# An attention and feed-forward block on one core: iterations written out, weight splits spread over iterations, rotation tables made in later groups, preparation reordered

## The chip, the cores and the metric

One NeuronCore of a Trainium2 chip. The time is device microseconds (us) of one execution. Engines by the profile's names: PE is the matrix engine (PEld its weight loads), ACT the scalar engine, DVE the vector engine, POOL GpSimd, SP the engine that issues most DMAs.

## The reference, cut to what matters

```python
x = x + layernorm(attn(layernorm(x)))     # x: 8 images of 512 tokens x 256
x = x + layernorm(ffn(layernorm(x)))
# attn, 16 heads of 64 complex numbers; t is the token
q, k, v = complex projections of x;  qr, kr = q * phase, k * phase   # phase = exp(i * t * omega)
E = exp(clip(-mu * |t_i - t_j|, -30, 0))
s = real(qr @ conj(kr));  qn, kn = |q|^2, |k|^2
V = sigma2 / (2 mu) * (1 - E * E) + eta2 + gamma2
maha = max(qn + E*E*kn - 2*E*s, 0) / V
logits = -0.5*tau*(nu+64) * log1p(maha / nu) - 32 * log(V), causal
out = softmax(logits) @ v;  y = out @ Wo
# ffn: silu(x @ Wg) * (x @ Wu) @ Wd, 256 -> 768 -> 256, integer weights
```

Everything is in float32. A projection is made from three products of high and low parts, so weights and inputs are split into `hi` (rounded to the matrix engine's format) and `lo = x - hi`.

## The kernel before, in words

The 16 heads are taken in 8 groups of 2 heads; a group goes over the 8 images. One *iteration* is one image in one group, 64 in all, numbered t. An iteration's program is software-pipelined: each engine, in a fixed order written by hand in its `body`, works on the present image (`c`), finishes the one before (`cp`) and begins the next (`cn`). In PE's order, an iteration has `project` (L786), `scores` (L826), `turn` (L838, transposes of the probabilities), `attend` (L850), `values` (L816) and `out_project` (L861). ACT squares projections (L1169), takes `log` (L1186) and `exp` (L1194), and copies PSUM results (`keep_turned` L1201, `keep_values` L1180, `keep_norm_k` L1175). DVE has `rotate` (L1488), `decay` (L1596), `distance` (L1607), `logits` (L1615), `add_output` (L1639). POOL has `sum_squares` (L600), `rotated` (L608) and `decay_norm` (L618). Engines meet only by semaphores; the order on each is the program's.

How the iterations are issued: `run_iterations` writes out t = 0 to 8. Groups 1 to 6 stand in an outer hardware loop of three rounds with two groups each; inside a group, iterations 1 to 4 are an inner loop of two rounds with two iterations each. Group 7 comes after the outer loop. In looped code the counts that semaphores are compared with are registers, and `settle` adds a semaphore increment on DVE ahead of each `distance` and `logits`.

A group needs its own weights and tables. SP loads the raw weights of the next group into the `lo` half of `wt` and the tables into `tabs` of the other parity. In each of the iterations j = 5 and 6 of a group, ACT turns three 256-column slots into `hi` with one instruction (`high_weights`, L374) at the start of its body, and POOL subtracts them one by one at three places (`low_weights`, L379).

The rotation tables (cos, sin, -sin of t * omega, 4 heads a set, 4 sets `ROPES`) are all made in t = 0: DVE makes the reduced angles with 5 instructions a set (L1460 to L1469), ACT the sines and cosines with 4 (L1125 to L1130), and SP stores them to DRAM, from where a group's table is loaded. Layer-norm statistics of the images (`x_stats`, L1506) are taken for images 4, 5 and 6, 7 in pairs, in t = 0 and t = 1. The feed-forward weights are cast from integers (`ffn_cast_of`, L1153, on ACT), transposed on PE (`ffn_turn`, L751) and copied out by ACT (`ffn_keep`, L1149): 9 turns, 4 of them ahead of t = 0 and 5 in it. After t = 63 the feed-forward part runs.

## Time and profile before

| | us |
|---|---|
| median of 3 runs (1907.66 to 1908.88) | 1907.91 |
| the profiled execution | 1907.7 |
| its span, first to last instruction | 1905.9 |
| PE busy | 1798.5 (94%) |
| DVE busy | 1609.2 (84%) |
| ACT busy | 1578.6 (83%) |
| POOL busy | 1453.4 (76%) |

The table is read as shares of the whole span. Stages differ: preparation up to the start of t = 0 (some 50 us), then 64 iterations, then the feed-forward part of some 190 us. The rows below cut the span into iterations, at the starts of the `values` products (L816).

### The profile page before, as it was taken

Reading aid. Unit: us, or ns where it says so; the run is one execution under the profiler, and the core shown is the slowest. Engines: PE = TensorE matmul, PEld = TensorE weight load, DVE = VectorE, ACT = ScalarE, POOL = GpSimd, SP = SyncE. Lnnn points to the kernel's source line nnn. Section 1 sums busy time; section 2 is a strip of 40 time slices with the busy share of each in tenths; the row PEclk is TensorE's granted clock in tenths of the full one; section 3 lists DMA queues with packets and bytes.
Section 4 is the critical chain, followed back from the end, with each engine's and each line's share of the span. In section 5 each row is a group of like instructions: output and inputs, shape, how many; then the busy total and the mean of one; then the engine's idle time right before and its main releaser. Section 6 shows DMA issues by size and latency. Waiting matters only on the chain.

```text
span 1905.9 us, 40909 instructions
## 1 busy us (share of the span) xinstructions
PE 1798.5 (94%) x10672; PEld 1477.9 (78%) x10672; DVE 1609.2 (84%) x3842; ACT 1578.6 (83%) x3224; POOL 1453.4 (76%) x1288
## 2 busy tenths in 40 slices
PE   4589999999999999999999999999999999998997
PEld 3377788887888887887888778887888788876876
DVE  7788898888888887888888878888888888996884
ACT  5779888898888887888888888888888888886664
POOL 5367788888888887888888877888888888872663
PEclk8799999999999999999999999999999999999998
DMA  7313101231122111311013111211131111010111
GB/s 210 119 40 111 62 24 44 78 94 45 45 78 88 33 42 47 110 62 46 33 69 94 46 47 64 89 43 46 45 111 45 46 45 42 26 54 14 45 45 45
DMA packets 61087, 117.72 MB, mean 62 GB/s; under 512 B 13488, under 2 KB 42928, under 8 KB 52704
## 3 DMA queue, kind: packets, MB, share of 16 engines
q1 hardware_dynamic: 59936, 115.51, 18.0%
q8 instruction: 78, 1.28, 0.3%
q14 instruction: 113, 0.93, 0.2%
q10 hardware_dynamic: 960, 0.00, 0.0%
HBM read 99.64 MB, written 21.36 MB: 63 GB/s over the span
## 4 chain that ended last, share of the span: by engine, by line
PE 60%; DVE 10%; POOL 8%; issue 6%; ACT 2%; DVEq 0%; POOLq 0%; ACTq 0%
PE pa L786 13%; PE ps L826 11%; PE py L850 10%; PE po L861 9%; PE pp L816 7%; PE pp L838 5%; POOL qk L608 4%; PE pa L797 3%; PE pa L805 2%; DVE lg L1607 2%; DVE stats L1645 1%; POOL ek L618 1%; DVE ps L1596 1%; DVE lg L1615 1%; DVE acc L1667 1%
## 5 line engine op out<-in xcount | busy, mean ns | idle before, releaser
L608 POOL TENSOR_TENSOR qk<-rm 64x512 f32<-64x512 f32 x504 | 684.2, 1357 | 102.7 <-PE ps L826 44.2
L618 POOL TENSOR_TENSOR ek<-tabs,kn 128x512 f32<-128x512 f32 (+3 forms) x512 | 460.7, 906 | 151.7 <-DVE lg L1607 112.1
L1615 DVE CUSTOM_DVE_ANT_0 lg<-lg,tabs,ncog 128x512 f32<-128x512 f32 (+3 forms) x512 | 442.6, 883 | 0.6 <-issue 0.6
L786 PE MATMUL pa<-xt,wt 128*128 128x512 f32 x1488 | 424.4, 421 | 12.5 <-issue 6.9
L826 PE MATMUL ps<-qk 128*128 128x512 f32 (+3 forms) x1024 | 375.0, 450 | 25.0 <-DVE lg L1607 24.9
L1488 DVE TENSOR_TENSOR rm<-pa,tabs 128x512 f32<-128x512 f32 x504 | 327.9, 678 | 70.8 <-POOL qk L608 65.7
L1607 DVE CUSTOM_DVE_ANT_0 lg<-ps,ek,qb 128x512 f32<-128x512 f32 (+3 forms) x512 | 279.5, 546 | 125.3 <-POOL ek L618 82.7
L850 PE MATMUL py<-pt,vt 128*128 128x128 f32 x2560 | 347.9, 275 | 0.1
L850 PEld LDWEIGHTS py<-pt,vt 128*128 128x128 f32 x2560 | 330.6, 191 | 16.5 <-issue 0.3
L786 PEld LDWEIGHTS pa<-xt,wt 128*128 128x128 f32 x1488 | 275.9, 193 | 66.1 <-issue 11.2
L1186 ACT ACTIVATE lg<-lg,qb 128x512 f32<-128x512 f32 (+3 forms) x512 | 278.5, 558 | 19.4 <-DVE lg L1607 15.9
L1194 ACT ACTIVATE pr<-lg,nmax 128x512 f32<-128x512 f32 (+3 forms) x512 | 283.3, 554 | 1.5
L861 PE MATMUL po<-wot,yt 128*128 128x256 f32 x1024 | 271.3, 388 | 6.1 <-DVE acc L1637 3.1
L1596 DVE TENSOR_TENSOR ps<-ps,tabs 128x512 f32<-128x512 f32 (+3 forms) x512 | 250.1, 489 | 23.8 <-PE ps L826 22.4
L1201 ACT ACTIVATE pt<-pp 128x512 f32<-128x512 f32 (+3 forms) x512 | 219.1, 430 | 59.2 <-PE pp L838 40.9
L861 PEld LDWEIGHTS po<-wot,yt 128*128 128x128 f32 x1024 | 180.3, 191 | 84.3 <-DVE acc L1639 42.2
L838 PEld LDWEIGHTS pp<-ident,pr 128*128 128x128 f32 x1280 | 164.0, 141 | 80.2 <-issue 44.0
L1639 DVE SCALAR_TENSOR_TENSOR acc<-po,rden,acc 128x256 f32<-128x256 f32 (+1 forms) x480 | 208.0, 474 | 16.4 <-PE po L861 16.4
L1169 ACT ACTIVATE sq<-pa 128x512 f32<-128x512 f32 x256 | 151.6, 593 | 82.4 <-PE pa L786 82.2
L838 PE MATMUL pp<-ident,pr 128*128 128x128 f32 x1280 | 214.2, 274 | 4.1 <-ACT pr L1194 2.3
L600 POOL TENSOR_TENSOR sq<-sq 128x512 f32<-128x512 f32 x126 | 161.9, 1285 | 54.8 <-ACT sq L1169 54.7
L826 PEld LDWEIGHTS ps<-qk 128*128 128x128 f32 x1024 | 161.0, 192 | 48.6 <-DVE lg L1607 41.1
(193 smaller groups left out, 2245.2 us busy)
## 6 DMA issues: line engine op xcount, KB each, us to landing
xt<-xs_d SPq DMA_DIRECT2D x56, 1024.0 KB, 4.8
tabs<-vec_d SPq DMA_DIRECT2D x7, 1536.0 KB, 9.6
xs_d<-xt SPq DMA_DIRECT2D x6, 1024.0 KB, 4.0
wt<-wraw_d SPq DMA_DIRECT2D x7, 768.0 KB, 5.6
acc<-in_L_attn_x SPq DMA_DIRECT2D x8, 512.0 KB, 6.0
tabs<-in_L_attn_x SPq DMA_DIRECT2D x8, 512.0 KB, 4.9
out<-tabs SPq DMA_DIRECT2D x8, 512.0 KB, 3.1
tabs<-rope_d SPq DMA_DIRECT2D x56, 64.0 KB, 4.1
```

What stands on the lines that cost most here:

```text
L608: pool.tensor_tensor(qk[part * DH:(part + 1) * DH, z * HH + hh, :], rm[row, 2 * part, :], rm[row, 2 * part + 1, :], ALU.add if part else A ...
L618: pool.tensor_tensor(ek[:, n % 2, 0:w], tab(par, hh, E2_T, w), kn[:, hh, 0:w], ALU.mult).then_inc(ek_pool, 1)
L786: last = mm(pa[r][:, :], wproj(par, z, kt, a, r * P, (r + 1) * P), xbuf[x][:, kt, b, :], start=(n == 0), stop=(n == 3 * KT - 1))
L826: mm(ps[n % 2][:, 0:w], qk[:, hh, TILES[n] * P:(TILES[n] + 1) * P], qk[:, HH + hh, 0:w], start=True, stop=True).then_inc(s_rdy, 1)
L838: last = pe.transpose(pp[i][:, j * P:(j + 1) * P], pr[:, hh, o:o + P], ident[:, :])
L850: last = mm(py[:, I * P:(I + 1) * P], vt[:, slot, j, hh * P:(hh + 1) * P], pt[:, i, j * P:(j + 1) * P], start=(j == 0), stop=(j == I))
L861: last = mm(po[:, jj * D:(jj + 1) * D], yt[:, hh, j * P:(j + 1) * P], wot[:, par, hh * D:(hh + 1) * D], start=True, stop=True)
L1186: act.activation(lg[:, hh, at(n)], lg[:, hh, at(n)], ACT.Ln, bias=qb[:, slot, 1, q:q + 1]).then_inc(ln_act, 1)
L1194: act.activation(pr[:, hh, at(n)], lg[:, hh, at(n)], ACT.Exp, bias=nmax[:, q:q + 1], scale=-1.0, accum_out=den[:, q:q + 1]).then_inc(ex_ac ...
L1488: tt(rm[:, m, :], pa[r][:, :], ropet(par, m in (IS, RS)), ALU.mult).then_inc(mul_dve, 1)
L1607: dve._custom_dve(bass.dve_ops.TENSOR_ADD_SAT, out=lg[:, hh, at(n)], in0=ps[n % 2][:, 0:w], in1=ek[:, n % 2, 0:w], s0=3e38, s1=qb[:, slot, ...
L1615: dve.tensor_tensor_reduce(lg[:, hh, at(n)], lg[:, hh, at(n)], tab(par, hh, T3_T, w), ncog[:, par, 0, hh:hh + 1], 3e38, ALU.add, ALU.min, ...
```

## The change

1. `run_iterations` writes out all 64 iterations on each engine; there are no loops, registers or `settle`. Counts are constants.
2. The weight split: one slot an iteration. ACT takes one 256-column slot after its second `log`, POOL subtracts it after `decay_norm(c, 1, 0)`. Groups 1 to 6 do this in j = 1 to 6, group 0 in j = 2 to 6 (two slots in the last). SP loads the raw weights at j = 0 (group 0: j = 1), the output weights one iteration later with a semaphore of their own.
3. Rotation tables: set 0 is made in t = 0. Sets 1, 2, 3 are made in groups 1, 3, 5, in the buffer that the next group's tables will take: DVE's five instructions in j = 1, 2, 3, ACT's sines in j = 3 and cosines in j = 4; SP stores them at j = 4, and then loads the next group's tables (before: at j = 2 and 3).
4. Preparation: `mu` is loaded and used first, the norm constants (`nco`) go out before the decay vectors, the small column arithmetic on DVE is ahead of the first rotations, `x_stats` goes by one image (images 4 to 7 in t = 0 to 3), and the feed-forward casts and turns are spread: 1 cast and 2 turns ahead of t = 0, 2 casts and 7 turns in it. The first raw weights lie in other buffers.

```diff
-        def run_iterations(eng, body):
-            for t in range(B + 1):
-                body(whole(t))
...
-            with eng.Fori(0, G // 2 - 1) as gg:
-                group(gg, 1, False)
-                group(gg, 0, False)
-            group(G // 2 - 1, 1, True)
+        def run_iterations(body):
+            for t in range(G * B):
+                g, j = divmod(t, B)
+                if g == G - 1:
+                    split = ()
+                elif g == 0:
+                    split = (j - 2,) if 2 <= j < 6 else (4, 5) if j == 6 else ()
+                else:
+                    split = (j - 1,) if 1 <= j < 7 else ()
+                if g == 0:
+                    rope = (0, 0) if j == 0 else None
+                else:
+                    rope = ((g + 1) // 2, j) if g % 2 and g < G - 1 and 1 <= j < 5 else None
...
 ACT body
-                if it.raw is not None:
-                    act.wait_ge(w_in[1 - it.par], it.raw)
-                    high_weights(act, 1 - it.par, 3 * it.part, 3 * it.part + 3).then_inc(w_hi, 1)
...
                 log(c, 0, 2, it.slot)
+                for g, q in it.split:
+                    high_weights(act, g, q)
...
                 keep_values(c, it.slot, 1)
-                if it.own == 1:
-                    for k in range(ROPES):
-                        rope_trig(k)
-                    act.wait_ge(rope_act, 4 * ROPES + 3)
+                if it.rope == (0, 0):
+                    rope_sines(0)
+                    rope_cosine(0)
+                    act.wait_ge(rope_out[0], 48)
+                elif it.rope is not None and it.rope[1] == 3:
+                    rope_sines(it.rope[0])
+                elif it.rope is not None and it.rope[1] == 4:
+                    rope_cosine(it.rope[0])
                 log(c, 1, 3, it.slot)
...
 DVE body
                 decay(c, 1, 2, it.par)
+                if it.rope is not None and it.rope[1] == 1:
+                    angle_turns(it.rope[0])
+                if it.rope is not None and it.rope[1] == 2:
+                    angle_first(it.rope[0])
+                if it.rope is not None and it.rope[1] == 3:
+                    angle_clamp(it.rope[0])
                 if nxt:
                     rotate(cn, it.behind, 1, RC)
...
-                if it.own == 1:
-                    all_angles_ready()
-                    for k in range(ROPES):
-                        rope_angle(k)
-                if it.own in (1, 2):
-                    x_stats(it.own + 2)
...
                 decay(c, 1, 3, it.par)
+                if it.own is not None and it.own < 5:
+                    x_stats(it.own + 3)
+                if it.rope is not None and it.rope[1] == 1:
+                    angle_whole(it.rope[0])
+                if it.rope is not None and it.rope[1] == 2:
+                    angle_second(it.rope[0])
                 distance(c, 1, 3, it.slot)
```

Where instructions stand. POOL, iteration j = 5 of a looped group before: the three subtractions L379 (`wt`) among `rotated` (qk), `sum_squares` (sq) and `decay_norm` (ek).

```order
L618 TENSOR_TENSOR ek<-tabs,kn 128x512 [waits x_dve]
L377 ISA
L379 TENSOR_TENSOR wt<-wt 128x256 [waits w_hi]
L599 REGISTER_ALU
L600 TENSOR_TENSOR sq<-sq 128x512 [waits sq_act]
...
L608 TENSOR_TENSOR qk<-rm 64x512 [waits s_rdy,mul_dve,rot_pool1]
L379 TENSOR_TENSOR wt<-wt 128x256 [waits w_hi,rot_pool1]
```

The same place on POOL now, in one of the iterations j = 1 to 6 of group 1: one subtraction (now L346), with no register instructions around it.

```order
L593 TENSOR_TENSOR ek<-tabs,kn 128x128 [waits x_dve,rot_pool1]
L593 TENSOR_TENSOR ek<-tabs,kn 128x512 [waits x_dve,kn_act]
L346 TENSOR_TENSOR wt<-wt 128x256 [waits w_hi]
L575 TENSOR_TENSOR sq<-sq 128x512 [waits sq_act]
L583 TENSOR_TENSOR qk<-rm 64x512 [waits s_rdy,mul_dve,sum_pool]
```

Two of the three subtractions of such an iteration have moved to other iterations; the one that stays stands ahead of `sum_squares`.

ACT at the end of an iteration in a looped group before: `exp`, `keep_values`, then `log` (1, 3) and `keep_turned` (0, 0), whose output `pt` PE's next `turn` waits for.

```order
L1194 ACTIVATE pr,den<-lg,nmax 128x512 [waits rd_dve,tr_rdy,f_dve]
L1180 ACTIVATE vt<-pp 128x512 [waits v_rdy]
L1186 ACT_TABLE_LOAD
L1186 ACTIVATE lg<-lg,qb 128x128 [waits x_dve]
L1201 ACTIVATE pt<-pp 128x512 [waits av_rdy,tr_rdy]
```

The same place now in j = 3 and then in j = 4 of group 1 (groups 3 and 5 alike): sines, and cosines by way of the absolute value, each with an activation-table load of their own.

```order
L1163 ACTIVATE vt<-pp 128x512 [waits v_rdy]
L1104 ACT_TABLE_LOAD
L1104 ACTIVATE tabs<-tabs 128x512 [waits rope_dve]
L1105 ACTIVATE tabs<-tabs 128x512
L1169 ACT_TABLE_LOAD
L1169 ACTIVATE lg<-lg,qb 128x128 [waits x_dve]
L1184 ACTIVATE pt<-pp 128x512 [waits av_rdy,tr_rdy]
...
L1163 ACTIVATE vt<-pp 128x512 [waits v_rdy]
L1111 ACTIVATE tabs<-tabs 128x512 [waits rope_act]
L1113 ACT_TABLE_LOAD
L1113 ACTIVATE tabs<-tabs,half_pi 128x512 [waits rope_act]
L1169 ACT_TABLE_LOAD
```

Two instructions and one more table load now stand ahead of `log` (1, 3) and `keep_turned` (0, 0), in six of the 64 iterations.

## Rows read from the trace of the kernel before

**Rows 1.** Stretches: us, busy (count) of PE, PEld, DVE, ACT, POOL, clock, DMA, GB/s.
```profile
57.90:115.70 57.80, 37.37 (x191) 27.74 (x190) 49.12 (x109) 43.28 (x84) 30.62 (x26) 0.82 0.29 105
115.70:147.90 32.20, 28.14 (x164) 22.75 (x162) 28.38 (x73) 25.24 (x54) 22.25 (x19) 0.95 0.09 34
147.90:175.30 27.40, 26.50 (x163) 21.72 (x162) 24.63 (x55) 24.89 (x53) 20.66 (x18) 1.00 0.25 97
281.70:306.80 25.10, 25.07 (x156) 20.76 (x154) 22.41 (x53) 22.23 (x47) 20.96 (x19) 1.00 0.12 43
407.30:485.00 77.70, 76.21 (x458) 62.22 (x458) 66.76 (x158) 67.73 (x141) 65.81 (x61) 1.00 0.16 52
713.30:743.90 30.60, 26.98 (x156) 21.94 (x154) 22.11 (x53) 22.47 (x47) 20.61 (x19) 0.94 0.11 38
1125.20:1156.50 31.30, 28.02 (x156) 22.72 (x154) 22.05 (x53) 22.43 (x47) 20.57 (x19) 0.89 0.11 37
1588.00:1613.10 25.10, 25.10 (x156) 20.74 (x154) 22.07 (x53) 22.30 (x47) 20.66 (x19) 1.00 0.12 42
1638.20:1664.20 26.00, 25.56 (x156) 20.84 (x154) 23.34 (x53) 22.32 (x47) 20.48 (x19) 1.00 0.11 41
```

**Rows 2.** Chain that ended last, 720 to 728 us: start, us, what.
```profile
724.12 3.62 issue
```

**Rows 3.** Source lines of the weight split: durations ns min/median/max, first and last start.
```profile
L374 ACT ACTIVATE wt<-wt x14: 827/829/833, 214.8 to 1473.1; 128x768 fp32r<-128x768 f32 x14
L379 POOL TENSOR_TENSOR wt<-wt x42: 725/734/789, 217.2 to 1492.8; 128x256 fp32r<-128x256 f32 x42
```

**Rows 4.** Timeline of a plain iteration: start, us, what, [idle before <-releaser].
```profile
1598.20 0.58 ACT L1201 ACTIVATE pt<-pp 128x512 f32<-128x512 f32 x1
1600.01 0.38 PE L838 MATMUL pp<-ident,pr 128*128 128x128 f32 x2
1600.91 0.51 ACT L1186 ACTIVATE lg<-lg,qb 128x256 f32<-128x256 f32 x1
1602.03 0.60 ACT L1169 ACTIVATE sq<-pa 128x512 f32<-128x512 f32 x1 [0.61 <-PE pa L786]
1602.71 1.28 POOL L600 TENSOR_TENSOR sq<-sq 128x512 f32<-128x512 f32 x1 [0.47 <-ACT sq L1169]
1610.05 2.64 POOL L608 TENSOR_TENSOR qk<-rm 64x512 f32<-64x512 f32 x2 [0.64 <-PE ps L826]
1611.46 0.69 DVE L1488 TENSOR_TENSOR rm<-pa,tabs 128x512 f32<-128x512 f32 x1 [1.02 <-POOL qk L608]
```

**Rows 5.** Timeline of the preparation and of t = 0.
```profile
39.38 1.27 ACT L1175 ACTIVATE kn<-pa,ncog 128x512 f32<-128x512 f32 x2 [3.07 <-DVE ncog L1800]
48.88 1.47 ACT L1153 ACTIVATE tabs<-tabs 128x1536 f32<-128x1536 int32 x1
54.33 0.43 DVE L1596 TENSOR_TENSOR ps<-ps,tabs 128x256 f32<-128x256 f32 x1 [7.96 <-PE ps L826]
76.63 1.57 DVE L1460 TENSOR_SCALAR yt<-wot,om 128x512 f32<-128x512 f32 x1
81.59 1.28 ACT L1125 ACT_TABLE_LOAD   x1
93.91 1.65 PE L826 MATMUL ps<-qk 128*128 128x384 f32 x2 [12.63 <-DVE lg L1607]
```

**Rows 6.** Source lines of the rotation tables on ACT.
```profile
L1126 ACT ACTIVATE tabs<-yt x1: 614/614/614, 85.7 to 85.7; 128x512 f32<-128x512 f32 x1
L1130 ACT ACTIVATE tabs<-pt,half_pi x4: 721/722/722, 84.6 to 91.5; 128x512 f32<-128x512 f32 x4
```

**Rows 7.** Page: DMA issues, KB each, median us from issue to landing.
```profile
rope_d<-tabs SPq DMA_DIRECT2D x11, 256.0 KB, 2.4
```

**Rows 8.** Timeline of t = 61: DVE's logits beside POOL's product.
```profile
1655.61 1.01 POOL L618 TENSOR_TENSOR ek<-tabs,kn 128x384 f32<-128x384 f32 x1
1655.63 1.53 DVE L1615 CUSTOM_DVE_ANT_0 lg<-lg,tabs,ncog 128x512 f32<-128x512 f32 x1
```

More of the change, by code:

```diff
@@ L26 @@
 ACT = mybir.ActivationFunctionType
-It = namedtuple("It", "t half b par slot before behind b_before new opens raw part ready fresh own x xn over")
+It = namedtuple("It", "t half b par slot before behind b_before opens split own x xn over rope")
+Rope = namedtuple("Rope", "turns ang sp sn om om2")
 B, N, D = 8, 512, 256
@@ L200, in build @@
         w_in = [sem(f"w_in{i}") for i in range(2)]
+        wo_in = [sem(f"wo_in{i}") for i in range(2)]
         w_stage = [sem(f"w_stage{i}") for i in range(3)]
@@ new lines, in run_iterations @@
+        def run_iterations(body):
[11 more added lines that the diff above has]
+                    rope = ((g + 1) // 2, j) if g % 2 and g < G - 1 and 1 <= j < 5 else None
+                body(It(t=t, half=t // 2, b=j, par=g % 2, slot=t % 2, before=(t - 1) // B % 2 if t else None,
+                        behind=(t + 1) // B % 2 if t + 1 < G * B else None, b_before=(t - 1) % B,
+                        opens=g + 1 if j == B - 1 and g < G - 1 else None, split=[(g + 1, q) for q in split],
+                        own=t + 1 if t + 1 < B else None, x=t % XBUF if g == 0 else t % 2,
+                        xn=(t + 1) % XBUF if t + 1 < B else (t + 1) % 2, over=t <= B, rope=rope))
@@ L658, in body @@
                     rotated(cn, 0, 1, 1)
-                if it.raw is not None:
-                    low_weights(pool, 1 - it.par, 3 * it.part + 1, it.ready)
                 if nxt:
@@ L1715, in body @@
                 if it.opens is not None:
-                    dve.wait_ge(grp[it.behind], it.opens)
-                    start(it.fresh, it.behind)
+                    dve.wait_ge(grp[it.behind], 16 * TABLE_LOADS * (it.opens // 2 + 1))
+                    start(it.opens, it.behind)
+                if it.rope == (0, 0):
+                    angle_turns(0)
+                    angle_whole(0)
                 decay(c, 0, 3, it.par)
                 distance(c, 0, 3, it.slot)
-                if it.own in (2, 3):
-                    x_move(it.own + 1)
+                if it.own is not None and 1 <= it.own < 6:
+                    x_move(it.own + 2)
                 if old:
@@ L1776, in body @@
                 decay(c, 1, 3, it.par)
+                if it.own is not None and it.own < 5:
+                    x_stats(it.own + 3)
[3 more added lines that the diff above has]
+                    angle_second(it.rope[0])
                 distance(c, 1, 3, it.slot)
```

456 lines of the change are left out of this document (214 added, 242 removed).

## The prediction

> **What bounds the kernel now.** I read the busy time by iteration first, then the chain of waits at the two odd iterations, then the timeline of one plain iteration and of the preparation. In a plain iteration (1588.0 to 1613.1) PE is busy 25.10 of 25.10 us at full clock, while ACT and DVE have 22.3 and 22.1 [rows 1]. PE is the bound, and such an iteration can only get longer. What is above 25.1 is what a change can take away:
>
> - Three iterations of a looped group, t = 13 to 15, take 77.7 us, that is 77.7 − 3 × 25.1 = 2.4 above three plain ones [rows 1]. These hold the weight splits: POOL is busy 65.8 us there against 3 × 20.66 = 62.0. The same pattern comes in groups 1 to 6.
> - Two iterations, at 713.3 and 1125.2, take 30.6 and 31.3 us [rows 1], 5.5 and 6.2 too long, where each engine goes back to the top of the outer loop. The chain there is 3.62 us of "issue", time without work or a wait that the profile knows [rows 2], and PE's mean clock over the iteration is 0.94 and 0.89 of full, 2.4 GHz, against 1.00 elsewhere [rows 1]. It had idled just before the clock fell to its lower level, 1.2 GHz.
> - From the start of t = 0 to the `values` of t = 1 (57.9 to 115.7) PE is busy for 37.4 of 57.8 us [rows 1], and stands still for 12.63 of them in one piece [rows 5]. The next iteration takes 32.2, the one after 27.4 [rows 1].
>
> **The loops.** The outer loop's back edge goes: 5.5 + 6.2 = −11.7 us. The inner loops cost nothing now (a looped plain iteration is 25.1 and the written-out one at 281.7 is 25.1 too [rows 1]), so removing them and `settle` gives nothing by itself. What is late next at these two places is PE itself. Bounds: −11.7 to 0 (if straight code of this length stalled as often).
>
> **The weight splits.** Removed: 6 × 2.4 = −14.4. What returns: ACT's slot of 256 columns, between a third of 0.83 us and the whole of it [rows 3]; it stands behind the `log` that ends at 1601.42, where ACT waits 0.61 for PE [rows 4], so I take nothing. POOL's 0.73 [rows 3] stands where POOL waits 0.47 for ACT [rows 4], so `sum_squares` comes 0.26 later; POOL waits for PE again for 0.64 at 1610.05, ahead of the rotation for which DVE then waits [rows 4]. So I take 0.1 an iteration, 36 iterations: +3.6. Bounds: 0, and the old price of a third of 2.4/2 = 1.2, 0.4 an iteration, +14. Queued behind the new wait for `w_hi` is POOL's `sum_squares`, for which DVE's and PE's next work waits. I take 3.6 and not the upper bound because the old form had three subtractions in an iteration, two of them at places without a wait.
>
> **The rotation tables in groups 1, 3, 5.** ACT's end of an iteration gets, in j = 3, one table load of 1.28 [rows 5] and two sines, 0.61 each [rows 6], some 0.1 less as they overlap: 2.4. In j = 4: an absolute value (0.61), a wait, a load of 1.28 and 0.72 [rows 6]: 2.7. Behind them wait `log` (1, 3) and `keep_turned` (0, 0). The latter ends at 1598.78, and PE's `turn`, which needs its buffer, starts at 1600.01 [rows 4]: slack 1.2. So PE, which has none itself, loses 2.4 − 1.2 = 1.2 and 2.7 − 1.2 = 1.5: 2.7 a group, +8.1 for three. Bounds: 0 (if DVE and POOL ran ahead so that PE could be given other work, which its fixed order excludes; so hardly) and the full 5.1 a group, +15.
> DVE's five instructions a group stand where DVE waits for POOL: 1.02 us at 1611.46 [rows 4], and as much ahead of the last `distance`. But they also meet POOL's work: the first such instruction in the old t = 0 took 1.57 us [rows 5], in the company of a POOL product. I take +1 a group, +3. Bounds 0 and, at about 1 us excess for each of the fifteen (1.57 against the 0.6 of an ACT pass over the same tile [rows 6]), +15.
> The Trainium skill, "SBUF — State Buffer", section "Who interferes with whom", speaks against this part: a DVE instruction in a two-port mode, or with two SBUF inputs, and a GpSimd instruction that reads SBUF shut each other out for a whole instruction. The 1.57 us agrees. By that rule alone each of the 15 instructions would wait for a POOL product to end.
>
> **Preparation and group 0.** (a) `kn` waited 3.07 us for `nco` [rows 5]; `start` now stands ahead of two statistics: −3. (b) DVE waited 7.96 us at 54.33 for scores that stood behind two casts of 1.47 us on ACT and four turns [rows 5]: −8. The two casts and two of the turns with their copies return inside t = 0, where ACT is the busy engine: 2 × 1.47 + 2 × 0.6 = +4. (c) At t = 0 ACT's rotation block reaches from 81.59 to the end of the next table load, which starts with PE's scores at 93.9: 95.2 [rows 5], 13.6 us. Now: load 1.28, sines 1.2, absolute value and cosine 1.4, and the wait until the three stores have landed, 2.4 to land [rows 7] and an estimated 1.3 for the issue of three: 7.6. ACT: −6. DVE's block beside it (from 76.63 [rows 5] to just before those scores) shrinks to one image's statistic and five spread instructions, so that DVE and POOL no longer begin after ACT: the 12.63 of PE could go in full. I take −8. Sum of (a) to (c): −15, bounds −5 and −21.
> (d) In t = 1 two more images' statistics stood ahead of `add_output`, for which PE waited: 32.2 against 27.4; now −4, against +1 for one image's statistic in each of t = 1 to 3 (an estimate: about 2 us of DVE where it has 1 us idle [rows 4]), and −0.5 for the splits: −1.5.
>
> **Phases.** The iterations that were written out already (t = 7, 8, 61, 62) lack `settle`; t = 61 took 26.0 us [rows 1]. There POOL's product began 0.02 us ahead of DVE's logits, which took 1.53 us for 512 columns [rows 8], and DVE is busy 23.3 us in the iteration against 22.1 in the plain one [rows 1]; t = 7 took 25.1. One in some iterations may fall this way: I take +2, bounds 0 and 0.9 × 48 = +43.
>
> **Sum**, on the profiled execution (1907.7; the span of 1905.9 and 1.8 around it, 0.2 below the median): 1907.7 − 11.7 − 14.4 + 3.6 + 8.1 + 3 − 15 − 1.5 + 2 = 1881.8, say 1882.
>
> **Rivals.**
> - The splits are wholly hidden and the preparation gives its upper bound: 1882 − 3.6 − 5 − 2 (no phase cost) − 3 = 1868. For: POOL's 0.64 and ACT's 0.61 of waiting are there [rows 4]. Against: the first iterations have DVE and ACT both near 25 of 27.4 [rows 1]. Chance 0.17.
> - The preparation doesn't give: ACT, with 2 casts and 7 turns in t = 0, becomes its bound, and (a) to (c) are −5: 1892; with splits at twice my price 1896. For: ACT is busy 43.3 of 57.8 [rows 1] with less in it. Chance 0.16.
> - The change doesn't do what it says: instruction supply stalls straight code too, so that the 11.7 come back elsewhere: 1894. Against: t = 0 to 8 and the feed-forward part are straight code, and the interval at 281.7 has PE busy for 25.07 of 25.1 [rows 1]. Chance 0.05. (The Trainium skill, "Runtime: NRT & Kernel Launch", section "Instruction fetch mechanics", has the same: straight code is fetched ahead, a taken branch out of the window is not.)
> - Slower: without `settle`, DVE and POOL arrive in t = 61's order in most iterations, 0.9 us each. Beyond 26/0.9 = 29 of the 55 iterations from t = 8 on this eats the whole gain; with 48 it is 1880 + 43 = 1923. For: t = 61 itself. Against: t = 7, 8 and 62 are written out and plain [t = 7: rows 1]. Chance 0.05.
> - The forecast as summed, own range 1874 to 1890: 0.57.
>
> **Numbers.** 1882. 8 in 10 lie between 1866 and 1897. 0.2% of the time, 3.8 us, is about what a measurement can tell. Faster holds all cases but the last, and the tail of the second: 0.93; same 0.03; slower 0.04.
>
> **What the profile would show.** No iteration of 30 us after t = 1, clock 1.00 from about t = 2 on; if one is left, the loop step is wrong. j = 5, 6, 7 of each group at 25.1 to 25.3; if all of j = 1 to 6 show 25.5, the split costs its bound. In groups 1, 3, 5, two iterations of about 26.5 with PE's `turn` waiting for ACT's `pt`; if they are 25.1 the slack was larger, if 27.6 smaller. `kn` near 36 us, and PE's longest wait in t = 0 at 5 us or less. Many logits of 1.5 us in plain iterations would be the slower rival. I would be wrong if the plain iteration, t = 58 say, were not 25.1.

## The result, and the profile after

The changed kernel takes 1877.28 us (median of 4 runs, 1874.37 to 1878.49), the kernel before 1908.06 beside it (1907.66 to 1908.88): ratio 0.9837, 95% interval 0.9824 to 0.985. The forecast was 1882, between 1866 and 1897. The profiled run took 1878.49, with a span of 1876.7 against 1905.9. Its engines:

```profile
PE 1792.1 (95%) x10672; PEld 1476.5 (79%) x10672; DVE 1628.9 (87%) x3848; ACT 1580.4 (84%) x3259; POOL 1469.7 (78%) x1291
```

TensorE has the same 10672 matmuls and 6.4 us less busy time than before (1798.5); the other 23 us of the span were standstill. The stretches of the trace after, that answer to [rows 1] (same columns). The first is from the start of t=0 (VectorE's last piece of the first logits) to the `values` of t=1; then from there to the `values` of t=2; the two stretches that begin at the `values` of j=3 and j=4 of group 1; three stretches with splits in group 2; the place of the first back edge; the stretch that the prediction calls t=61, which read 26.0 before; and the part from the last `values` to the end:

```profile
46.20:101.10 54.90, 42.75 (x223) 32.84 (x222) 40.28 (x88) 42.21 (x80) 33.78 (x29) 0.90 0.33 122
101.10:129.50 28.40, 27.06 (x162) 21.69 (x161) 26.53 (x65) 25.30 (x54) 22.30 (x20) 1.00 0.18 66
366.00:392.70 26.70, 25.46 (x155) 20.67 (x154) 22.17 (x53) 24.50 (x51) 21.45 (x20) 1.00 0.12 41
392.70:419.50 26.80, 25.47 (x155) 20.69 (x154) 22.18 (x53) 24.60 (x51) 21.49 (x20) 1.00 0.55 177
595.50:670.80 75.30, 75.22 (x459) 62.34 (x458) 67.22 (x158) 66.90 (x141) 63.95 (x57) 1.00 0.26 81
695.90:721.00 25.10, 25.06 (x155) 20.78 (x154) 23.70 (x54) 22.45 (x48) 21.57 (x20) 1.00 0.21 74
1606.50:1631.70 25.20, 25.17 (x156) 20.86 (x154) 22.51 (x53) 22.22 (x47) 21.05 (x19) 1.00 0.13 43
1679.80:1876.70 196.90, 167.38 (x948) 143.64 (x946) 133.96 (x370) 109.22 (x212) 91.28 (x72) 0.94 0.12 38
```

The kernel before has this last part in 193.6 us, with the same instructions but a higher mean clock, 0.97 instead of 0.94:

```profile
1712.30:1905.90 193.60, 164.09 (x948) 140.88 (x947) 133.96 (x370) 109.22 (x212) 91.31 (x72) 0.97 0.13 39
```

The ruler for all that follows is the start of TensorE's `values` line in each iteration, v(0) to v(63). The stretch of t is v(t) to v(t+1), and "t=61" stays the prediction's name for v(60) to v(61). In the profiled execution of each kernel (us; "low" is the time at the clock's lower level behind v(63), without the last 8 to 9 us, which every execution has). Up to v(1), kernels with the same code differ by up to 1.7 us (97.9 to 99.6 in e7, e10, e11, e12; 101.1 to 101.7 in after, e3, e4, e8, e9), so a small difference there is no result:

| kernel | v(0) | v(1) | v(8) | v(63) | end | v(63) to end | low |
|---|---|---|---|---|---|---|---|
| before | 70.2 | 115.7 | 306.8 | 1712.3 | 1905.9 | 193.6 | 6.8 |
| after | 67.1 | 101.1 | 290.5 | 1679.8 | 1876.7 | 196.9 | 17.0 |
| e1_unroll_only | 71.6 | 116.6 | 307.8 | 1695.5 | 1889.9 | 194.4 | 10.2 |
| e2_split_together | 67.4 | 101.6 | 291.5 | 1689.3 | 1884.3 | 195.0 | 13.6 |
| e3_rope_no_tables | 67.5 | 101.7 | 291.2 | 1672.4 | 1867.4 | 195.0 | 13.6 |
| e4_keep_first | 68.0 | 101.3 | 290.6 | 1680.0 | 1872.9 | 192.9 | 6.8 |
| e5_outer_only | 70.6 | 116.3 | 307.5 | 1694.9 | 1889.4 | 194.5 | 10.2 |
| e6_casts_ahead | 69.1 | 105.5 | 294.9 | 1684.2 | 1880.9 | 196.7 | 17.0 |
| e7_store_free | 67.0 | 98.3 | 287.7 | 1676.9 | 1869.9 | 193.0 | 6.8 |
| e8_one_event | 68.4 | 101.6 | 291.0 | 1677.0 | 1869.9 | 192.9 | 6.8 |
| e9_start_late | 67.4 | 101.6 | 290.7 | 1679.9 | 1873.7 | 193.8 | 6.8 |
| e10_combined | 68.2 | 99.6 | 289.0 | 1675.0 | 1871.9 | 196.9 | 17.0 |
| e11_best | 68.3 | 97.9 | 287.1 | 1673.2 | 1866.1 | 192.9 | 6.8 |
| e12_tail_busy | 67.7 | 99.1 | 288.5 | 1674.4 | 1867.6 | 193.2 | 6.8 |

So of the 29.2 us of span: −16.3 until v(8) (−14.6 of it until v(1)); from v(8) to v(63) −16.2, made of −11.6 at the back edges (30.53 and 31.28 to 25.1 each), −14.6 at the iterations that held the splits (2.44 in each of six groups), −0.9 at t=61, and +11 of new costs, nearly all in groups 1, 3, 5; and +3.3 behind v(63).

### The profile page after: what moved, and what is told of

Its sections match the earlier page's. It is cut to its first block, busy times and chain, and to the rows that moved or that the text cites. A ratio compares the mean times of both kernels' runs of the same rounds, so it can differ in the third digit from the quotient of the medians.

```text
span 1876.7 us, 35392 instructions
## 1 busy us (share of the span) xinstructions
PE 1792.1 (95%) x10672; PEld 1476.5 (79%) x10672; DVE 1628.9 (87%) x3848; ACT 1580.4 (84%) x3259; POOL 1469.7 (78%) x1291
## 4 chain that ended last, share of the span: by engine, by line
PE 72%; DVE 10%; ACT 4%; issue 3%; POOL 1%; DVEq 0%; POOLq 0%; ACTq 0%
PE pa L759 15%; PE py L823 13%; PE ps L799 12%; PE po L834 10%; PE pp L789 8%; PE pp L811 6%; PE pa L770 4%; PE pa L778 2%; DVE lg L1603 2%; DVE stats L1630 1%; DVE rm L1472 1%; DVE acc L1652 1%; DVE tabs L1690 1%; DVE lg L1596 1%; POOL rstd L602 1%
## 5 line engine op out<-in xcount | busy, mean ns | idle before, releaser
L583 POOL TENSOR_TENSOR qk<-rm 64x512 f32<-64x512 f32 x504 | 697.2, 1383 | 93.2 <-PE ps L799 49.1
L799 PE MATMUL ps<-qk 128*128 128x512 f32 (+3 forms) x1024 | 366.5, 442 | 7.8 <-DVE lg L1596 7.6
L823 PEld LDWEIGHTS py<-pt,vt 128*128 128x128 f32 x2560 | 331.7, 192 | 16.2 <-issue 0.3
L1169 ACT ACTIVATE lg<-lg,qb 128x512 f32<-128x512 f32 (+3 forms) x512 | 273.0, 557 | 14.4 <-DVE lg L1596 10.4
L1624 DVE SCALAR_TENSOR_TENSOR acc<-po,rden,acc 128x256 f32<-128x256 f32 x480 | 207.9, 474 | 17.7 <-PE po L834 17.4
L789 PE MATMUL pp<-wt,xt 128*128 128x256 f32 x1488 | 193.6, 286 | 2.7 <-ACT pt L1184 2.0
```

What stands on the lines that cost most here:

```text
L583: pool.tensor_tensor(qk[part * DH:(part + 1) * DH, z * HH + hh, :], rm[row, 2 * part, :], rm[row, 2 * part + 1, :], ALU.add if part else A ...
L789: last = mm(pp[half][:, jj * W2:(jj + 1) * W2], xbuf[x][:, kt, a, j * P:(j + 1) * P], wproj(par, 2, kt, b, 0, W2), start=(n == 0), stop=(n ...
L799: mm(ps[n % 2][:, 0:w], qk[:, hh, TILES[n] * P:(TILES[n] + 1) * P], qk[:, HH + hh, 0:w], start=True, stop=True).then_inc(s_rdy, 1)
L823: last = mm(py[:, I * P:(I + 1) * P], vt[:, slot, j, hh * P:(hh + 1) * P], pt[:, i, j * P:(j + 1) * P], start=(j == 0), stop=(j == I))
```

## Experiments: the loops and the splits

**e1_unroll_only.** The kernel before, its 64 iterations written out, nothing else.

```
-            with eng.Fori(0, G // 2 - 1) as gg:
-                group(gg, 1, False)
-                group(gg, 0, False)
-            group(G // 2 - 1, 1, True)
+            for g in range(1, G):
+                for k in range(0 if g > 1 else 1, B):
+                    body(It(t=g * B + k, ...))      # numbers in place of registers
```

> The kernel before with its 64 iterations written out and nothing else changed. Theory (the loop's turns cost what the idle time and the lower clock behind them show): the six stretches of 30.53 to 31.3 us between two starts of the first values() line become 25.1 to 25.3 like the plain ones, two of them gone in full (6.2 and 5.4 us), so 11 to 12 us less than before: about 1896 us. The stretches with weight splits stay at 25.25, 26.17 and 26.31 us. Rival A (straight code starves the engines of instructions): new idle time of TensorE shows that nothing releases, and the total stays within 3 us of before. Rival B (written-out code lets VectorE and GpSimd settle in the other order that iteration 61 of before shows): many plain stretches read 25.9 instead of 25.1, and the total is above 1905 us.

1891.70 us (1890.95 to 1893.62), ratio to before 0.9922 (0.9908 to 0.9936): 16 us gone, where theory said 12. (Two stretches, not six, were of 30 us; the expectation's first clause miscounts.) A split iteration, the first back edge's place, and the one odd stretch that is left:

```profile
433.30:459.10 25.80, 25.22 (x156) 20.79 (x154) 22.72 (x53) 22.63 (x48) 22.84 (x22) 1.00 0.12 42
712.20:737.30 25.10, 25.07 (x155) 20.77 (x154) 22.40 (x53) 22.12 (x47) 20.96 (x19) 1.00 0.13 43
1141.60:1167.70 26.10, 25.63 (x156) 20.88 (x154) 23.59 (x53) 22.16 (x47) 20.62 (x19) 1.00 0.12 41
```

Rivals A and B fall: no new standstill, and the other order of DVE and POOL came once (v(41) to v(42); DVE busy 23.59 for 22.4), while t=61 became plain. What no theory had: the three split stretches of a group fell from 25.25, 26.17, 26.31 to 25.12, 25.77, 25.79, so 1.06 a group or 6.4 in six belonged to the loop and not to the splits.

**e5_outer_only.** Which loop? The kernel before with `for gg in range(G // 2 - 1)` for the outer `Fori`; the inner loops stay.

> The kernel before with only its outer loop (two groups a turn, three turns) written out; the inner loops of four plain iterations stay, and so do the registers that they count with. Theory A (the split iterations of before cost 2.44 us a group where the same work costs 1.38 in straight code, because wait values that hang on the outer loop's register are computed there by each engine; and the outer loop's jumps are what stalls): no stretch of 30 us, the split stretches fall to 25.12, 25.77 and 25.79 us, total near 1892 like the kernel with everything written out. Theory B (the 1.06 us a group is what leaving an inner loop costs, late): the 30 us stretches go, but the split stretches stay at 25.25, 26.17 and 26.31 us: total near 1897. Rival C (the stall belongs to the inner loops): the two stretches of 30.5 and 31.3 us stay: 1908.

1891.59 us (1890.23 to 1893.57), ratio 0.9911 (0.9896 to 0.9926), the same as with everything written out: theory A. No stretch of 30 us is left; a split iteration, and t=61:

```profile
432.90:458.70 25.80, 25.22 (x155) 20.78 (x154) 22.73 (x53) 22.63 (x48) 22.85 (x22) 1.00 0.11 42
1620.80:1646.80 26.00, 25.56 (x155) 20.84 (x154) 23.36 (x53) 22.30 (x47) 20.47 (x19) 1.00 0.11 41
```

The inner loops, their jumps and their registers, cost nothing where TensorE is the bound; t=61 keeps its 26.0 with them. What the outer loop's registers cost can be read off POOL in a split iteration, where it is short of time. First the kernel before (start, us, ..., idle before it), then e1_unroll_only at the same place:

```profile
451.23 1.34 POOL L618 TENSOR_TENSOR ek<-tabs,kn 128x384 f32<-128x384 f32 x1
452.79 1.33 POOL L608 TENSOR_TENSOR qk<-rm 64x512 f32<-64x512 f32 x1 [0.22 <-POOL ek L618]
454.27 0.73 POOL L618 TENSOR_TENSOR ek<-tabs,kn 128x256 f32<-128x256 f32 x1 [0.16 <-POOL qk L608]
```

```profile
451.87 1.34 POOL L599 TENSOR_TENSOR ek<-tabs,kn 128x384 f32<-128x384 f32 x1
453.29 1.47 POOL L589 TENSOR_TENSOR qk<-rm 64x512 f32<-64x512 f32 x1
454.84 0.73 POOL L599 TENSOR_TENSOR ek<-tabs,kn 128x256 f32<-128x256 f32 x1
```

Between two products that wait for each other lie 0.22 and 0.15 us with a register as the value waited for (451.23 + 1.34 = 452.57 to 452.79), 0.08 with a constant. From the one split at the head of an iteration to the next POOL takes 26.18 us (432.19 to 458.37) against 25.79 (433.07 to 458.86), which is the difference of the iterations. In e5 the gaps are 0.08 in the split iterations, whose values are constants there, and stay at 0.15 to 0.23 in the inner loops, so they do go with the registers. That the 0.39 consists of them is not shown: in these three rows the middle product takes 0.14 longer with constants, and only 0.07 of the two gaps is left (3.04 from the first start to the third, against 2.97). `settle` went out of the split iterations by the same edit, and no run tells its share.

**e2_split_together.** The changed kernel with the splits as before.

```
-                    split = (j - 1,) if 1 <= j < 7 else ()
+                    split = (0, 1, 2) if j == 5 else (3, 4, 5) if j == 6 else ()
+                    act.activation(hi[:, q:q + 3, :], lo[:, q:q + 3, :].bitcast(F32), ACT.Copy).then_inc(w_hi, 3)
```

> The changed kernel with the weight splits of the kernel before: per group one ScalarE cast of three slots at the start of the bodies j=5 and j=6, and GpSimd's three subtractions at three places in each; all else as changed. Theory: the three stretches behind them take 25.25, 26.17 and 26.31 us again, 2.44 us more per group over plain ones in six groups, so 14.6 us over the changed kernel, about 1892 us; in group 0 the image stretches may add up to 2 us. Rival A (the splits were hidden, and what was lost there came from somewhere else, such as the loop's bookkeeping registers): the stretches stay at 25.1 to 25.3 and the total within 2 us of the changed kernel. Rival B (only GpSimd's part counts, so that placing them early in groups 1, 3, 5 clashes with nothing): 7 us.

1886.25 us (1884.46 to 1888.66), ratio 0.9893 (0.9879 to 0.9907): 9.0 us over the changed kernel's median, and 9.5 at v(63). Neither 14.6 nor 2 nor 7. The stretches behind j=5 and j=6 of group 2:

```profile
623.10:648.90 25.80, 25.20 (x154) 20.76 (x153) 22.73 (x53) 22.62 (x48) 22.85 (x22) 1.00 0.12 41
648.90:674.70 25.80, 25.22 (x155) 20.78 (x154) 22.69 (x54) 22.01 (x47) 22.11 (x21) 1.00 0.11 42
```

0.7 each, 1.4 a group, 8.3 in six groups: the same as in e1_unroll_only. (The rest of the 9.5 is there by v(8) for the most part: 291.5 against 290.5.) The splits and the outer loop shared the 14.6 as 8.3 and 6.4. One split an iteration is free: in the changed kernel they are

```profile
L341 ACT ACTIVATE wt<-wt x42: 401/402/416, 115.6 to 1444.2; 128x256 fp32r<-128x256 f32 x42
L346 POOL TENSOR_TENSOR wt<-wt x42: 722/778/794, 116.6 to 1445.1; 128x256 fp32r<-128x256 f32 x42
```

and the 75.30 us for three of them above are three plain iterations (25.08, 25.10, 25.10). Two splits in one iteration are not free. Group 0 takes two in its j=6, and in the changed kernel the stretch with both reads 25.6 (25.56), 0.46 over a plain one:

```profile
214.70:240.30 25.60, 25.36 (x156) 20.80 (x154) 23.13 (x53) 22.78 (x49) 22.25 (x21) 1.00 0.27 83
```

## Experiments: the rotation tables of groups 1, 3, 5

ACT and TensorE in the changed kernel at the end of j=3 of group 1:

```profile
374.66 1.28 ACT L1104 ACT_TABLE_LOAD   x1
375.96 0.63 ACT L1104 ACTIVATE tabs<-tabs 128x512 f32<-128x512 f32 x1
376.49 0.61 ACT L1105 ACTIVATE tabs<-tabs 128x512 f32<-128x512 f32 x1
377.12 1.28 ACT L1169 ACT_TABLE_LOAD   x1
378.73 0.58 ACT L1184 ACTIVATE pt<-pp 128x512 f32<-128x512 f32 x1
379.45 0.41 PE L811 MATMUL pp<-ident,pr 128*128 128x128 f32 x2 [1.20 <-ACT pt L1184]
```

377.12 − 374.66 = 2.46 us are put in, and the iteration loses 26.72 − 25.10 = 1.62; at j=4 it is 2.7 and 1.69. The second load is there in any iteration, since the logarithm needs it behind the exponentials.

**e3_rope_no_tables.** `ACT.Copy` and `ACT.Identity` for `ACT.Sin` in groups 1, 3, 5 (sines and cosines of heads 4 to 15 left out).

> The changed kernel with the three activations of each rotation table in groups 1, 3 and 5 done as Copy, Copy and Identity, so that no table of ScalarE is loaded for a sine; their place, size and waits stay. It leaves out the sines and cosines of heads 4 to 15, whose tables then hold plain angles. Theory (ScalarE's work at that place is what TensorE waits for through the probabilities' copy): two loads of 1.28 us per event go, leaving 1.2 to 1.3 us of ScalarE work; TensorE's waits of 1.2 to 1.3 us at the transposes disappear, the two stretches per event group of 26.7 and 26.8 us fall to 25.1 to 25.4, and the total falls by 8 to 10 us, to about 1868. Rival (VectorE's five rotation instructions, stretched to 1.5 to 1.8 us beside GpSimd, are what costs): both stretches stay at 26.5 to 26.8 and the total stays.

1869.16 us (1867.99 to 1872.73), ratio 0.9805 (0.9791 to 0.9819).

```profile
366.70:392.00 25.30, 25.27 (x155) 20.72 (x154) 22.75 (x54) 23.11 (x50) 21.53 (x20) 1.00 0.12 44
392.00:417.50 25.50, 25.45 (x155) 20.68 (x154) 22.60 (x53) 23.30 (x50) 21.51 (x20) 1.00 0.59 186
```

TensorE's wait for `pt` is gone, 1.42 and 1.28 us with it (26.72, 26.79 to 25.30, 25.51): the price of the one load, 1.28, passed on whole. (The expectation counted two loads; the one of L1169 stayed.) The rival falls: VectorE's five instructions, three of them drawn out (in the changed kernel; the third is L1452, again 1.53),

```profile
312.64 1.53 DVE L1432 TENSOR_SCALAR tabs<-tokens,om 128x512 f32<-128x512 f32 x1
337.74 1.79 DVE L1442 SCALAR_TENSOR_TENSOR tabs<-tokens,om,tabs 128x512 f32<-128x512 f32 x1
```

against 0.49 for L1432 at the start of t=0 (47.49), leave stretches of 25.10, 25.10 and 25.30: 0.2 a group.

**e4_keep_first.** The copy that TensorE waits for, ahead of the sines:

```
+                early = it.rope is not None and it.rope[0] > 0 and it.rope[1] in (3, 4)
+                if early:
+                    keep_turned(c, 0, 0)
+                    (rope_sines if it.rope[1] == 3 else rope_cosine)(it.rope[0])
```

> The changed kernel with one call moved in groups 1, 3 and 5 alone: ScalarE keeps the turned probabilities of tile (0,0) before it makes the sines (j=3) or the cosine (j=4), and not behind them. Theory (ScalarE's own order, with that copy queued behind the sines, is what holds TensorE): the wait at the transposes falls from 1.2 and 1.3 us to nothing or to what the next reader of ScalarE waits for (the squares that come behind); each of the six stretches loses 0.4 to 1.6 us, so 3 to 9 us in all, about 1872 us. Rival (the sum of ScalarE's work in such a stretch is the bound, its order not): the stretches stay at 26.7 and 26.8, the wait only moves to another line, and the total stays within 1 us of 1877.

1876.16 us (1874.65 to 1876.66), ratio 0.9839 (0.9825 to 0.9853); the stretches stay at 26.72 and 26.78, v(63) at 1680.0. The rival is right.

```profile
374.69 0.60 ACT L1184 ACTIVATE pt<-pp 128x512 f32<-128x512 f32 x1
379.07 1.52 ACT L1169 ACTIVATE lg<-lg,qb 128x128 f32<-128x128 f32 x3
```

The copy now ends at 375.3, 4 us earlier (379.3 in the changed kernel), and TensorE's longest wait for it is 0.42 (at 383.34); but all behind the sines comes as late as before, and the time is lost to that. ACT works without a gap of 0.1 us from 372.6 to 382: the sum of its work is the limit, not the order.

**e8_one_event.** So fewer loads: in j=3 only the absolute value, in j=4 both sines and the cosine behind one load.

```
+            def rope_abs(k):      # j=3: needs no table
+                act.activation(z.turns, z.ang, ACT.Abs).then_inc(rope_act, 1)
+            def rope_all(k):      # j=4
+                act.activation(z.sp, z.ang, ACT.Sin).then_inc(rope_act, 1)
+                act.activation(z.sn, z.ang, ACT.Sin, scale=-1.0).then_inc(rope_act, 1)
+                act.activation(z.turns, z.turns, ACT.Sin, bias=half_pi[:, :], scale=-1.0).then_inc(rope_act, 1)
```

> The changed kernel with the rotation tables of groups 1, 3 and 5 made behind one table load in place of two: in j=3 ScalarE takes only the absolute value (it needs no load), in j=4 both sines and the cosine. Theory (ScalarE's extra time above a slack of about 1.0 us is what an iteration loses; today 2.5 and 2.7 us of extra work cost 1.62 and 1.69): j=3's stretch 25.1 to 25.3 us, j=4's 25.1 + 3.2 - 1.0 = 27.3 us, so 1.0 to 1.2 us less per group, 3 to 3.5 in all, about 1874 us. Rival (a block of 3.2 us holds back the logarithms behind it, so that VectorE and then TensorE lose it in full, slack or not): 28.3 us and no gain, 1877 us.

1871.74 us (1870.68 to 1877.37), ratio 0.9815 (0.98 to 0.9831).

```profile
366.50:391.60 25.10, 25.08 (x156) 20.78 (x154) 22.41 (x53) 22.82 (x49) 21.53 (x20) 1.00 0.13 44
391.60:418.90 27.30, 25.42 (x155) 20.67 (x154) 22.14 (x53) 25.12 (x52) 21.49 (x20) 1.00 0.53 173
```

25.10 and 27.31: 3.08 us put in (400.29 to 403.37), 2.21 lost; 1.1 a group or 3.3 saved, as theory had it. What ACT can take here without loss is thus 0.84, 0.99 and 0.87 us for additions of 2.46, 2.68 and 3.08; the 0.63 of the absolute value in j=3 cost nothing.

## Experiments: preparation and t=0

Rows of the changed kernel that answer to [rows 5]: `kn`, the logits that begin t=0, ACT behind the rotation block, and TensorE's longest wait in t=0.

```profile
36.99 1.27 ACT L1158 ACTIVATE kn<-pa,ncog 128x512 f32<-128x512 f32 x2 [2.40 <-issue]
46.20 0.48 DVE L1596 CUSTOM_DVE_ANT_0 lg<-ps,ek,qb 128x256 f32<-128x256 f32 x1 [1.57 <-issue]
83.12 0.40 ACT L1169 ACTIVATE lg<-lg,qb 128x128 f32<-128x128 f32 x1 [2.22 <-DMA rope_d<-pt]
84.15 0.66 PE L811 MATMUL pp<-ident,pr 128*128 128x128 f32 x2 [5.09 <-ACT pt L1184]
```

**e6_casts_ahead.** All three casts and four of the nine `ffn_turn` ahead of t=0, as before.

```
             ffn_cast_of(0)
+            ffn_cast_of(1)
+            ffn_cast_of(2)
             ffn_keep(0)
             ffn_keep(1)
+            ffn_keep(2)
+            ffn_keep(3)
```

> The changed kernel with the feed-forward weights made ready as in the kernel before: all three casts and four of the nine sets of turns ahead of t=0, five sets in t=0, at the places of before. Theory A (the prediction's: 8 us gained ahead, 4 returned inside t=0): the start of t=1's values at 105.1 instead of 101.1, about 1881 us. Theory B (the traces of before and after: the start of t=0 came 8.6 us earlier, 2.4 of them by kn, but 5.5 were given back until the first values, since ScalarE has the same work on either side of t=0): between 101 and 102.5, about 1878 us. Rival C (ScalarE in t=0 gets shorter by two casts and two copies, and those ahead hide behind waits for scores): earlier than 101, below 1876 us.

1882.85 us (1878.62 to 1883.09), ratio 0.9857 (0.9842 to 0.9872); v(1) at 105.5, 4.4 later: theory A in its sum. Not in its parts:

```profile
46.46 0.48 DVE L1595 CUSTOM_DVE_ANT_0 lg<-ps,ek,qb 128x256 f32<-128x256 f32 x1 [1.57 <-issue]
```

Here, with two casts more ahead of it, t=0 begins at 46.46, only 0.26 later. What had begun it 8.6 us late in the kernel before (54.79) was `scores(c0, 0, 2)` written behind the turns that waited for the casts; the change puts the scores first, and this experiment leaves them there. The casts and turns ahead of t=0 cost 2.0 until v(0) and 2.4 more until v(1).

**e7_store_free.** The negative sines into an empty buffer.

```
-        first_rope = rope_tiles((...), pt[:, 1, :], 0)
+        first_rope = rope_tiles((...), wot[:, 1, :], 0)
-                    act.wait_ge(rope_out[0], 48)          # ACT, t=0
+                    sp.wait_ge(rope_out[0], 48)           # SP, t=2, ahead of loading that buffer
```

> The changed kernel with one buffer changed: the negative sines of heads 0 to 3 are made in the still empty output-weight buffer of group 1 instead of the probabilities' buffer, so that ScalarE in t=0 no longer waits for the three stores of the tables to land; the sync engine waits for them in t=2, ahead of loading that buffer. Theory (that wait is on the path to the end): ScalarE's 2.22 us idle behind its table load at 79.6 disappear, TensorE's longest wait in t=0 falls from 5.1 to 2.9 us, and the start of t=1's values comes at 98.9 instead of 101.1: 2.2 us less in all, about 1875. Rival (the next limit is already there, for instance VectorE's logits with the statistic of an image beside them): less than 0.7 us less.

1875.19 us (1871.66 to 1876.58), ratio 0.9824 (0.9811 to 0.9838).

```profile
79.55 1.28 ACT L1171 ACT_TABLE_LOAD   x1
80.84 0.40 ACT L1171 ACTIVATE lg<-lg,qb 128x128 f32<-128x128 f32 x1
```

```profile
81.87 0.66 PE L813 MATMUL pp<-ident,pr 128*128 128x128 f32 x2 [2.90 <-ACT pt L1186]
```

ACT's 2.22 are gone and TensorE's 5.09 have become 2.90; v(1) is 2.8 earlier, v(63) 2.9. The four kernels with this edit reach v(1) at 97.9 to 99.6, those without it at 101.1 or later. The wait was on the path.

**e9_start_late.** `x_stats(2)` ahead of `start(0, 0)` in place of behind it.

> The changed kernel with VectorE's step start(0, 0), which copies the norms' coefficients for ScalarE's first kn, again behind the statistics of one image instead of ahead of them (in the kernel before it stood behind two images'). Theory (that order is what the prediction's 3 us came from, at half the size here, since it is one image and not two): kn about 2 us later than 36.99, and the start of t=0 and of t=1's values (101.1) 1 to 2 us later: about 1879 us. Rival (VectorE's work ahead of t=0 is the bound in either order, so that the copy comes later but the statistics earlier): values of t=1 within 0.5 us of 101.1, total unchanged.

1875.53 us (1875.11 to 1880.61), ratio 0.983 (0.981 to 0.9849). v(1) at 101.6, v(63) 1679.9: the rival.

```profile
35.39 0.15 DVE L1456 COPY ncog<-nco 128x6 f32<-128x6 f32 x1
```

```profile
37.32 1.27 ACT L1158 ACTIVATE kn<-pa,ncog 128x512 f32<-128x512 f32 x2 [2.69 <-issue]
```

The copy came 2.2 us later than in the changed kernel (33.18), `kn` 0.33. TensorE's norms, which `kn` reads, end at 36.9, so a copy at 35.4 is early enough. One image's statistics do no harm. In the kernel before, the copy came at 39.19, behind two images' statistics and behind small column arithmetic that now stands behind it:

```profile
33.58 0.87 DVE L1580 SCALAR_TENSOR_TENSOR pr<-kn,hp,pr 16x640 f32<-16x640 f32 x1
34.48 1.17 DVE L1581 TENSOR_SCALAR pr<-pr,hp 16x128 f32<-16x128 f32 x1
35.69 2.71 DVE L1506 BATCH_NORM_STATS2 stats<-acc 128x6 f32<-128x256 f32 x8
```

From the start of the statistics to the copy it took 3.5 us there and 2.17 in this run (33.22 to 35.39), so the halved statistics explain 1.3 of the 3.8 us between the two copies. The rest would be the arithmetic's; no run separates them.

## Experiments: adding up, and the part behind v(63)

**e10_combined.** e7's and e8's edits, with two more: the negative sines as a scaled copy of the sines in j=5, and no split in j=4 of groups 1, 3, 5.

```
+            def rope_negative(k):      # j=5
+                act.activation(z.sn, z.sp, ACT.Copy, scale=-1.0).then_inc(rope_act, 1)
+                    split = ((), (0,), (1,), (2,), (), (3,), (4, 5), ())[j] if g % 2 else ...
```

> The changed kernel with four edits: the negative sines of heads 0 to 3 in the empty output-weight buffer (2.8 us when done alone); one table load per rotation table, with the absolute value in j=3 (3.3 us alone); the negative sines of groups 1, 3, 5 as a scaled copy of the sines in j=5, inside ScalarE's slack there; and no weight split in j=4 of these groups (in j=6 two). Theory (ScalarE's slack of about 1.0 us an iteration takes what needs no load): j=4's stretch 25.1 + 1.28 + 0.53 + 0.65 - 1.0 = 26.5 us or, as the split of 0.3 is gone, 26.2; j=5 and j=6 at 25.1 to 25.2; with the other two edits 8 to 9 us less than the changed kernel, about 1869 us. Rival (the scaled copy and the later store of the tables cost what they save: the next group's tables come one iteration later, and TensorE or VectorE waits for them where the group changes): j=4 at 26.5 but a stretch of over 26 at the group's end, total 1871 or more.

1872.31 us (1869.11 to 1873.74), ratio 0.9801 (0.9782 to 0.9819). From v(1) to v(63) it takes the same 1575.3 us as the next run, which lacks the two added edits; together they gave nothing:

```profile
389.60:416.40 26.80, 25.44 (x155) 20.70 (x154) 22.16 (x53) 24.62 (x51) 21.49 (x20) 1.00 0.23 70
416.40:442.00 25.60, 25.34 (x155) 20.79 (x154) 23.12 (x53) 22.95 (x50) 22.24 (x21) 1.00 0.45 155
```

j=4 took 26.79, 0.52 less than 27.31, and j=5 25.58, 0.48 more. The reason lies in where the splits stand. The split that was dropped, j=4's, is done ahead of v(12) (381.57 in the changed kernel), in the stretch that had slack; the late stretch keeps the split of j=5 (405.34). And the two that were put together in j=6 fall in the stretch of j=5, beside the copy:

```profile
430.10 0.72 ACT L341 ACTIVATE wt<-wt 128x256 fp32r<-128x256 f32 x2
```

Group 0's stretch with two splits, shown above, has no copy and reads 25.56, with VectorE busy 23.13 and GpSimd 22.25, against 25.58, 23.12 and 22.24 here. So the 0.48 is the price of the second split, and the copy seems to have cost nothing. The copy by itself, which would then give 0.5 us a group, was not run. The tables' later loading did not cost: no stretch at the group's end is above 25.3.

**e11_best.** The changed kernel with e7's and e8's edits only.

> The changed kernel with two edits alone: the negative sines of heads 0 to 3 in the empty output-weight buffer, and one table load per rotation table with the absolute value in j=3. Theory (the edits act in different stretches, so their measured savings of 2.8 and 3.3 us add): the last values() line starts at 1673.7 instead of 1679.8 us, total 1871 us give or take 2 us for the clock in the feed-forward part. Rival (the saving of the first one is given back in group 0, which then meets its own limit): 1676 to 1677 for the last values() line, total 1874.

1869.92 us (1867.93 to 1872.13), ratio to before 0.9801 (0.9786 to 0.9816), and v(63) at 1673.2 as added up (theory: 1673.7); with v(1) at 97.9 where e7 had 98.3, the agreement is within what v(1) varies by. It beats both kernels; the changed one has 0.9837 (0.9824 to 0.985).

**e12_tail_busy.** The same kernel, with TensorE kept at work at the handover.

```
+            def idle_work(x, n):
+                for k in range(n):
+                    mm(pa[0][:, :], wproj(1, 0, 0, 0, 0, P), xbuf[x][:, 0, 0, :], start=True, stop=True)
```

> The kernel of the run above with 17 additional matmuls whose results nobody reads, put where TensorE stands still at the handover to the feed-forward part: 6 ahead of the second half of the last values (it waits 2.05 us there) and 11 ahead of the first feed-forward transposes (3.20 us); 1.6 and 3.0 us of work at full clock. Theory (TensorE's standstill at this place is what lowers its clock behind it, for 3.4 us in one execution and 10.2 in another, and so makes up to 4 us of the time and most of the spread between runs): no stretch of lower clock between the last values and 20 us later, the part from the last values to the end 193 us or less, the runs within 2 us of each other, and the median 1 to 3 us below the kernel without them. Rival (the clock falls there whatever TensorE does, or waits spread over a longer part of the tail lower it): the stretch stays, the time within 1 us or, where the matmuls delay what waits, up to 1 us more.

1869.19 us (1867.35 to 1869.58), ratio to before 0.979 (0.9776 to 0.9804). The question is the table's last two columns. In the changed kernel the worst piece is

```profile
1689.20:1699.40 10.20, 8.43 (x30) 7.07 (x31) 4.38 (x15) 5.57 (x11) 1.00 (x1) 0.50 0.00 0
```

at the lower level, 1.2 GHz; TensorE had stood still for 2.05 us (1681.4 to 1683.5), and was in the middle of 3.20 us of standstill (1686.8 to 1690.00) when it fell. With the added matmuls the two gaps were 0.66 and 0.68:

```profile
1675.91 1.55 PE L844 MATMUL pa<-xt,wt 128*128 128x512 f32 x6
1681.21 2.76 PE L844 MATMUL pa<-xt,wt 128*128 128x512 f32 x11
```

and no stretch of lower clock came within 150 us. But five other executions without them (e4, e7, e8, e11 entirely, e9 with 3.4 us there) escaped most of it too, and e11 has the same two waits, 2.05 and 3.20. What speaks for the theory is the spread of the five runs, 2.2 us, against 4.2 and 6.7 in e11 and e8, and their lack of a cluster 4 us higher; the median moved by 0.7 us, inside either interval. Not settled.

## Why the forecast held, step by step

- **Back edges, −11.7:** measured −11.6. The clock is back at 1.00 there, 2.4 GHz (the stretch at 695.90), and straight code of 64 iterations did not stall (e1). The rule of the Trainium skill in "Runtime: NRT & Kernel Launch", "Instruction fetch mechanics", agrees, for the outer loop's jump, in that a stall is there; the traces call it "issue" and don't show a fetch. The inner loops' jumps cost nothing (e5).
- **"Removing the loops gives nothing by itself" and splits −14.4:** the sum was right (−14.6 at those three stretches a group), the owner wrong. 6.4 of it are the outer loop's registers or the `settle` that comes with them (e1, e5), 8.3 the splits (e2). "Gives nothing by itself" was wrong for the iterations in which GpSimd is short of time. The sign was there to be seen: group 0, written out in the kernel before, has its split iterations at 25.78.
- **What the splits leave, +3.6:** nothing that can be seen. Three stretches of 25.2 to 25.3 (the last of group 1, one each in groups 2 and 4), +0.5 together, look like it. But e2 has the same three, though the splits stand elsewhere, and e9, with the splits where the changed kernel has them, has the one in group 2 plain:

```profile
570.60:595.70 25.10, 25.06 (x155) 20.78 (x154) 22.42 (x53) 22.44 (x48) 21.55 (x20) 1.00 0.12 43
```

  The term is mis-sized. GpSimd's waits of 0.47 and 0.64 [rows 4] took the 0.78 whole. The rival "the splits are wholly hidden" was right in this, though not in its total.
- **Rotation tables on ACT, +8.1:** +9.9 (1.62 and 1.69, three times). The slack is 0.84 to 0.99, not 1.2. TensorE's wait came where it was forecast, 1.20 and 1.29 for 1.2 and 1.5. Yet e4 shows that this wait was only the first place where the loss showed: the mechanism was the sum of ACT's work, not the copy queued behind it.
- **VectorE's part, +3:** +0.6. The instructions are drawn out as forecast (1.53 us), but where VectorE has time; the two shown began 0.03 us after a GpSimd product did (312.61 and 337.71). The rule of the Trainium skill in "SBUF — State Buffer", "Who interferes with whom", agrees with the durations; what they cost is read from the stretches.
- **Preparation, −15:** −14.6 at v(1), with parts that differ. `kn` 39.38 to 36.99, −2.4 for −3, not by `start`'s place (e9), but by what no longer stands ahead of it: half the statistics and, as read, the column arithmetic. Casts −4.4 (e6), the forecast's net of −8 and +4, but the −8 at the start of t=0 came from the scores' new place. TensorE's longest wait is 5.09 for 12.63; 2.2 of it were the stores' (e7). ACT's new block is 7.4 us (75.73 to 83.12) for the 7.6 worked out.
- **Group 0 behind v(1), −1.5:** −1.7 (189.4 for 191.1). t=1 fell from 32.2 to 28.4 and t=1 to 3 are each 1 to 1.6 above the 27.4 of before.
- **Phases, +2:** −0.9, as no stretch of the changed kernel reads like t=61 before, and the +0.5 of the three stretches above, whose cause stays open: −0.4. The slower rival had one case in e1 and none here.
- **Left out: the part behind v(63), +3.3.** The fourteen executions order by one number: 192.9 to 193.8 us with 6.8 of lower clock, 194.4 and 194.5 with 10.2, 195.0 twice with 13.6, 196.7 to 196.9 with 17.0: 0.35 us for each. It differs between runs of one kernel (the changed one's runs lie at 1874.4, 1876.1 and twice 1878.5), so it is hardly the change's. That those runs differ in this part was not looked at run by run; their mean clocks, 0.991 in the fastest and 0.988 in the others, agree with it.

Sum of the errors: back edges +0.1, splits −3.8 (−14.6 for −10.8), tables +1.8, VectorE −2.4, preparation +0.4, group 0 −0.2, phases −2.4, the end +3.3: −3.2, and 1881.8 − 3.2 = 1878.6 is the profiled run's 1878.5. That they cancel is luck: the four largest are 2 to 4 us each. But without the end's +3.3, which is hardly the change's, the sum would be 6.5 low, and 1875.3 is still inside the likeliest case's own range, as is the median of 1877.3. Most of the error lies in costs that were put in for caution and did not come.
